# An attention-and-experts kernel: the second layernorm's root, reciprocal and shift once for two blocks, and the expert numbers read into registers in two loads

## What is computed

```python
logits = x @ Wr + br
gate   = max(softmax(logits));  idx = argmax(logits)
xn     = layernorm(x) * ln_g + ln_b
h      = relu(xn @ W1[idx] + b1[idx])      # 128 -> 512
y      = (h @ W2[idx] + b2[idx]) * gate    # 512 -> 128
out    = layernorm(x + y)                  # (v - mean) / sqrt(var + 1e-5)
```

## Time and profile before

| | us |
|---|---|
| median of 3 timed runs | 200.94 |
| lowest, highest of them | 200.79, 201.41 |
| the profiled execution's own time | 202.25 |
| its span | 200.5 |
| busy in the span: PE, PEld, DVE, ACT, POOL | 147.8, 118.1, 161.1, 148.1, 114.3 |
| last DVE instruction starts | 191.4 |
| last OUT on ACT starts | 191.6 |
| last store on POOL starts | 193.4 |

### The profile page before, as it was taken

One profiled execution on the slowest core, in us unless ns is written; L12 is line 12 of the kernel. 1 busy time (PEld: TensorE's weight loads), 2 busy tenths in 40 slices (PEclk: granted clock), 3 DMA queues, 4 the chain that ended last, 5 costly groups with the idle time before them and its releaser, 6 DMA issues.

```text
span 200.5 us, 5489 instructions
## 1 busy us (share of the span) xinstructions
PE 147.8 (74%) x1446; PEld 118.1 (59%) x1446; DVE 161.1 (80%) x819; ACT 148.1 (74%) x448; POOL 114.3 (57%) x200
## 2 busy tenths in 40 slices
PE   0068979988997795922369878998998997999400
PEld 0015736857566474821316767987888996888200
DVE  2455287999998869699698899999999999799900
ACT  2358979997975696527645887999999999898520
POOL 4323140508789765634469215768677687578650
PEclk9999999999999998585556999999999999999955
DMA  5997184000101101101342212223222222110000
GB/s 131 346 394 261 26 273 159 3 0 15 40 26 35 42 29 41 54 15 40 77 126 83 56 30 55 66 71 76 65 75 64 66 64 69 53 54 19 28 9 0
DMA packets 16415, 15.74 MB, mean 79 GB/s; under 512 B 2810, under 2 KB 13142, under 8 KB 16386
## 3 DMA queue, kind: packets, MB, share of 16 engines
q1 hardware_dynamic: 14034, 11.10, 19.0%
q0 software_dynamic: 2272, 4.27, 6.4%
q10 hardware_dynamic: 80, 0.03, 0.1%
HBM read 10.52 MB, written 5.33 MB: 79 GB/s over the span
## 4 chain that ended last, share of the span: by engine, by line
PE 43%; DVE 33%; issue 8%; ACT 6%; DMA 3%; ACTq 2%; POOLq 1%; SPq 1%; POOL 0%; DVEq 0%
PE bank L473 7%; DVE hl L1239 6%; PE bank L592 6%; PE bank L430 5%; PE bank L445 4%; DMA XN<-in_attn_embeddings 3%; DVE z L1248 3%; PE bank L502 3%; PE bank L580 3%; PE bank L576 2%; PE bank L578 2%; DVE zpart L1244 2%; PE bank L579 2%; PE bank L595 2%; DVE bn L1252 2%
## 5 line engine op out<-in xcount | busy, mean ns | idle before, releaser
L418 POOL DMA_INDIRECT out<-OUT,tok x39 | 40.5, 1039 | 26.5 <-issue 25.0
L383 POOL DMA_INDIRECT rows<-R,place x32 | 31.8, 994 | 18.0 <-DVE place L919 9.4
L592 PE MATMUL bank<-W2hl,hh 128*128 x156 | 32.6, 274 | 7.0 <-issue 3.2
L576 PE MATMUL bank<-sel,bias 96*128 96x128 bf16 x156 | 34.6, 222 | 0.0
L578 PE MATMUL bank<-xh,W1h 128*128 128x128 f16 x156 | 34.2, 219 | 0.0
L580 PE MATMUL bank<-xh,W1l 128*128 128x128 f16 x156 | 34.1, 218 | 0.0
L579 PE MATMUL bank<-xl,W1h 128*128 128x128 f16 x156 | 34.0, 218 | 0.0
L1239 DVE SCALAR_TENSOR_TENSOR hl<-bank,hh 128x512 f16<-128x512 f32 x39 | 26.9, 690 | 3.5 <-ACT hh L746 2.6
L595 PE MATMUL bank<-W2hl,hl 128*128 x156 | 27.9, 219 | 0.0
L746 ACT ACTIVATE hh<-bank 128x512 f16<-128x512 f32 x39 | 23.1, 593 | 6.1 <-PE bank L580 5.8
L359 POOL TENSOR_TENSOR rmag<-guarded,minus_half 128x4 f32<-128x4 f32 x8 | 8.2, 1022 | 27.0 <-ACT guarded L615 27.0
(11 more groups left out here) (197 smaller groups left out, 459.3 us busy)
## 6 DMA issues: line engine op xcount, KB each, us to landing
XR<-rows SPq DMA_DIRECT2D x39, 66.0 KB
W<-in_ffn_W SPq DMA_DIRECT2D x1, 2048.0 KB, 11.0
X<-in_attn_embeddings SPq DMA_DIRECT2D x2, 512.0 KB, 8.6
X<-in_attn_embeddings SPq DMA_DIRECT2D x1, 768.0 KB
out<-OUT,tok POOLq DMA_INDIRECT x39
rows<-padt SPq DMA_DIRECT2D x9, 66.0 KB
XN<-in_attn_embeddings SPq DMA_DIRECT2D x2, 256.0 KB, 7.9
rows<-R,place POOLq DMA_INDIRECT x32
```

The lines of the kernel that those rows point to most:

```text
L383: pool.indirect_dma_start(out=rows[:, :], out_offset=bass.IndirectOffsetOnAxis(ap=place[u][:, k:k + 1], axis=0), in_=R[u][:, k, :], in_off ...
L418: pool.indirect_dma_start(out=out[:, :], out_offset=bass.IndirectOffsetOnAxis(ap=tok[k][:, 0:1], axis=0), in_=OUT[k][:, :], in_offset=None ...
L576: pe.matmul(h, bias3[:, c * P:(c + 1) * P], sel, start=True, stop=False)
L592: pe.matmul(y[:, 0:2 * D], hh[k][:, c * P:(c + 1) * P], w, start=c == 0, stop=False)
```

## The change

It does three things.

1. `sd` and `mv2` become tiles for two blocks (`GR = 2`). ACT takes the root, and DVE the reciprocal and the shift, once for both, 128x2 instead of 128x1, in the round in which the second of the two came up before. Block 38 has no partner and stays alone. Mean and variance (mv) are still made block by block.
2. Since the first block of a pair is now ready one round later, OUT on ACT and the store on POOL move by one round for every block: lead -4 instead of -3. The wait for the earlier store of the same buffer moves from the root to OUT.
3. PE reads the expert numbers in two loads, of 16 in front of block 0 and of 23 in front of y of block 12, into 39 registers. The loads in front of blocks 4, 20 and 28 go.

```diff
-            steps([(-3, store), (3, token)])
+            steps([(-4, store), (3, token)])
...
-            held_expert = [pe.alloc_register(f"expert{i}") for i in range(2 * UN)]
+            held_expert = [pe.alloc_register(f"expert{i}") for i in range(NB)]
...
-                if k == UN // 2 and (count(0) + 1) * UN < NB:
-                    if (count(0) + 1) * UN == NB1:
-                        pe.wait_ge(s["tabled"], TABLE_2)
-                    load_experts((count(0) + 1) * UN)
-
-            load_experts(0)
+                if count(0) * UN + k == NB1 - 4:
+                    pe.wait_ge(s["tabled"], TABLE_2)
+                    load_experts(NB1, NB2)
+
+            load_experts(0, NB1)
...
             def b_sd(count, k):
+                n = members(count, k)
+                if n:
+                    act.wait_ge(every["mv"], blocks(count(0), k))
+                    act.activation(sd[k // GR][:, 0, 0:n], mv2[k // GR][:, 0:n, 1], ACT.Sqrt, bias=epsc[:, 0:1]).then_inc(every["sd"], 1)
+
+            def b_fin(count, k):
                 after(act, stored[k], count(0) * 16)
-                act.wait_ge(every["mv"], blocks(count(0), k))
-                act.activation(sd[k][:, 0:1], mv2[k][:, 1:2], ACT.Sqrt, bias=epsc[:, 0:1]).then_inc(every["sd"], 1)
...
-            steps([(5, b_xs), (1, b_hh), (-3, b_fin), (4, b_xt), (-2, b_sd), (4, b_xh)])
+            steps([(5, b_xs), (1, b_hh), (-4, b_fin), (4, b_xt), (-2, b_sd), (4, b_xh)])
...
             def b_rec(count, k):
-                dve.wait_ge(every["sd"], blocks(count(0), k))
-                dve.reciprocal(sd[k][:, 1:2], sd[k][:, 0:1]).then_inc(every["rec"], 1)
+                n = members(count, k)
+                if n:
+                    dve.wait_ge(every["sd"], group(count, k))
+                    dve.reciprocal(sd[k // GR][:, 1, 0:n], sd[k // GR][:, 0, 0:n]).then_inc(every["rec"], 1)
```

More of the change, by code:

```diff
@@ L42 @@
 UN = 8
+GR = 2
 NB1, U1 = 16, 6
@@ L194, in build @@
         bn2 = [sb(f"bn2{i}", [P, 6]) for i in range(UN)]
-        mv2 = [sb(f"mv2{i}", [P, 2]) for i in range(UN)]
-        sd = [sb(f"sd{i}", [P, 3]) for i in range(UN)]
+        mv2 = [sb(f"mv2{i}", [P, GR, 2]) for i in range(UN // GR)]
+        sd = [sb(f"sd{i}", [P, 3, GR]) for i in range(UN // GR)]
         OUT = [sb(f"OUT{i}", [P, D]) for i in range(UN)]
@@ L254, in blocks, with members, group @@
             return turn * UN + k + 1
+        def members(count, k):
+            n = count(0) * UN + k
+            return n % GR + 1 if n % GR == GR - 1 or n == NB - 1 else 0
+        def group(count, k):
+            return (count(0) * UN + k) // GR + 1
         def pads(eng, first, n):
@@ L748, in b_sd @@
             def b_sd(count, k):
-                after(act, stored[k], count(0) * 16)
-                act.wait_ge(every["mv"], blocks(count(0), k))
-                act.activation(sd[k][:, 0:1], mv2[k][:, 1:2], ACT.Sqrt, bias=epsc[:, 0:1]).then_inc(every["sd"], 1)
-            def b_fin(count, k):
-                act.wait_ge(every["shift"], blocks(count(0), k))
-                act.activation(OUT[k][:, :], z[k][:, :], ACT.Identity, scale=sd[k][:, 1:2], bias=sd[k][:, 2:3]).then_inc(every["out"], 1)
-            steps([(5, b_xs), (1, b_hh), (-3, b_fin), (4, b_xt), (-2, b_sd), (4, b_xh)])
+                n = members(count, k)
[3 more added lines that the diff above has]
+            def b_fin(count, k):
+                after(act, stored[k], count(0) * 16)
+                act.wait_ge(every["shift"], group(count, k))
+                scale, shift = (sd[k // GR][:, row, k % GR:k % GR + 1] for row in (1, 2))
+                act.activation(OUT[k][:, :], z[k][:, :], ACT.Identity, scale=scale, bias=shift).then_inc(every["out"], 1)
+            steps([(5, b_xs), (1, b_hh), (-4, b_fin), (4, b_xt), (-2, b_sd), (4, b_xh)])
         @block.vector
@@ L1254, in b_mv @@
             def b_mv(count, k):
[L1256 to L1258 removed]
+                dve.wait_ge(every["bn"], blocks(count(0), k))
+                dve.bn_aggr(mv2[k // GR][:, k % GR, :], bn2[k][:, :]).then_inc(every["mv"], 1)
             def b_rec(count, k):
[L1261 to L1262 removed]
+                n = members(count, k)
+                if n:
+                    dve.wait_ge(every["sd"], group(count, k))
+                    dve.reciprocal(sd[k // GR][:, 1, 0:n], sd[k // GR][:, 0, 0:n]).then_inc(every["rec"], 1)
             def b_shift(count, k):
[L1265 to L1266 removed]
+                n = members(count, k)
+                if n:
+                    dve.wait_ge(every["rec"], group(count, k))
+                    stt(sd[k // GR][:, 2, 0:n], mv2[k // GR][:, 0:n, 0], -1.0, sd[k // GR][:, 1, 0:n], ALU.mult, ALU.mult).then_inc(every["shift"], 1)
             steps([(1, b_hl), (-1, b_mv), (0, b_z0), (-2, b_rec), (0, b_z), (-2, b_shift), (0, b_bn), (0, b_table), (4, b_xl), (4, b_split)])
```

7 lines of the change are left out of this document (3 added, 4 removed).

## The result

The changed kernel took **208.43 us** (median of four runs, 206.62 to 210.14) beside 201.18 for the kernel before. The ratio of the runs is 1.032, 95% interval [1.022, 1.042]; it leaves out the slowest, 210.14 us, which counts as a slow execution. Two later studies gave 1.0413 [1.0366, 1.0459] and 1.0291 [1.0233, 1.0349]. So it is slower, as forecast, but by 3 to 4% and not by 0.9%: 202.8 was predicted, and the range ended at 203.3.

A forecast was written before the change was run, and what follows sets the result against it. ACT was taken to set the pace of the steady rounds. Roots -0.3, loads -0.7, start +0.6, block 12 +1.0 and end +1.3 made +1.9 on 200.94, so 202.8 us; 8-in-10 range 200.5 to 203.3.

The forecast's parts named there:

- Reciprocal and shift: DVE, one of each fewer per two blocks: they run while DVE waits for its own results, so 0 us.
- Root: ACT, one root fewer per two blocks: 0.02 to 0.03 us a pair over about 12 pairs, -0.3 us.
- The end: POOL's last stores: four follow instead of three, 1.28 us apart, so the last starts later, +1.3 us.
- The start: First load, 16 numbers instead of eight, before block 0: longer load and register instructions, nothing hiding them, +0.6 us.
- Block 12: PE's load of 23 in front of y, its room already used up: the longer stall goes through, +1.0 us.
- Blocks 20 and 28: PE's loads removed there: stalls of 0.32 and 0.4 us go, 1.0 more taken as profile-only, -0.7 us together.
- Rival B: Block 28's long stall is in every run, so removing its load wins 1.0 us more: 201.8 us, chance 0.17.
- The move: OUT and store one round later: free in the middle, the token copy one store's time of about 1 us behind.
- Rival A: PE's loads take the same time whatever the number of registers: 201.6 us, chance 0.20.
- C: Load time independent of number, and block 28's 1.4 us stall in every run and removed: 200.5 us, chance 0.13.
- D: Fewer instructions save their whole place on DVE and ACT, 0.09 us a round, 2.2 us: 200.9 us, chance 0.10.
- two signs that I named for being wrong: Last store keeps its distance from hl of block 38, or the steady round gets shorter than 1.86 us.

The follow-up runs named there:

- pairs_16_tok_fours: Kernel before plus pairs and the later OUT and store, sixteen token-number buffers instead of eight, and expert loads of four throughout: ratio 0.9965.
- e9: Kernel before with expert numbers loaded four at a time throughout, the last load four instead of three: ratio 0.9919.
- e4: Kernel before with only OUT and the store one round later, roots block by block, loads of eight: ratio 1.0144.
- e1: Kernel before with only the two long loads of 16 and 23 expert numbers: ratio 1.0074.
- start_16_only: Kernel before with 16 expert numbers loaded at the start and 8, 8 and 7 at blocks 12, 20 and 28: ratio 1.0027.
- e2: Changed kernel with the five loads of the kernel before, so pairs and the later OUT and store alone: ratio 1.0146 in four runs.
- pairs_again: Changed kernel with the five loads of the kernel before, same as e2, measured again in a later study: ratio 1.0196.

## Why the prediction was wrong

The sign was right, and so was what the small operations are worth. By its own steps:

- **Reciprocal and shift: 0 forecast, 0 found.** zpart to z is 0.35 us without the reciprocal, as in the earlier trace rows.
- **Root: -0.3 forecast, -0.3 found** between hl of block 14 and 34 (37.41 us in pairs_16_tok_fours, 37.73 in e9), of which the last rounds give 0.1 back.
- **The end: +1.3 forecast, 1.34 found,** in every trace with pairs, by the step as told: one store more in the row of 1.28 us each. With single roots the move alone costs 0.75 there (e4), so the other 0.6 comes from the pairing: block 34's OUT waits for the pair's shift.
- **The start: +0.6 forecast,** 0.5 by the timed runs (1.0027, whose interval holds 0 to 1.2), 0.5 to 1.3 by the traces. Right in size.
- **Block 12: +1.0 forecast, +2.0 found** in round 14 (4.26 us in e1 against 2.26 in start_16_only), 3.5 where the clock falls. The mis-sized term is the load: "about 1.5 us" became 2.19. The slope of 0.055 a number came from one pair of rows, four and eight numbers on SP; on PE it is 0.07 to 0.08, and the three numbers beyond a multiple of four added 0.7 (20 take 1.51, 23 take 2.19).
- **Blocks 20 and 28: -0.7 forecast, -1.3 found** (44.97 us in e1 against 46.30 in start_16_only from hl of block 14 to 38). The step "I take it that this 1.0 us is missing in the timed runs" was wrong. The longest load was no accident of that execution: it is the one with seven numbers, and it was 1.09 to 1.17 us long in every kernel that kept it. Behind it the round of block 30 took 2.68 to 2.73 us in the five other traces, 0.8 over a round, so of the 1.41 us of the earlier trace rows some 0.8 is in every run and 0.6 was that execution's own, for a reason that is open. Rival B had half of it right.
- **The move: "In the middle this costs nothing" is the step that failed, and it carries most of the miss.** I saw that the token copy now stands one round behind the store that it waits for, and called the next store's own time of about 1 us enough. No row gave a landing time, and I put none in its place. It is 2.1 to 2.9 us and every fourth time 3.0 to 3.95, the copy comes 2.8 behind, and hh, which had 0.2 to 0.4 us of room behind the copy, passes the rest on to hl and the whole round. Found: +1.1 to +3.2 us between hl of block 14 and 38 (e2 and pairs_again against start_16_only), and in the changed kernel +1.2 to +3.8 against e1. In the timed runs the sixteen buffers take back 1.4 to 2.6%, 2.8 to 5.3 us, of the 3.9 to 6.4 us by which the sum was too low. In the first profiled execution, the fastest, the forecast for the profile was +0.9 and first load to last store took 4.3 longer. Of the 3.4 us between, 1.8 lie where the waits are (-0.56 from block 14 to 38 where the forecast had -0.3 - 1.7, and +0.39 ahead of block 13), 0.8 at block 12 and 0.7 at the start.

The sum with these sizes: start 0.6, block 12 and the two loads 0.7, the middle 1.2 to 3.8, the first rounds 0.4 (the wait of block 10), the end 1.3 makes 4.2 to 6.8, and a fall of the clock 1.5 more. The changed kernel was 5.8 to 8.3 us slower by its three ratios.

Rival A (no dependence on the number) is refuted by 0.33 us for four and 1.69 for 24 numbers; C fell with it, and D by pairs_16_tok_fours. Neither of the two signs that I named for being wrong came up, though the forecast was wrong: the last store is 1.3 us farther behind hl of block 38, and the undisturbed rounds average 1.865 us, not less than 1.86. The list of signs lacked the one that mattered, POOL's cg with idle time ended by a landing.

The Trainium skill, page Runtime: NRT & Kernel Launch, section Instruction fetch mechanics, has 200 ns a register, and the page's Terms describe such a load as reading from HBM; here the numbers lie in a tile in SBUF. In fours the runs show 0.07 to 0.08 us a number, and its figure is only near for the numbers left over. Estimated with 0.2 us a register the load of 23 would be 4.6 us; it was 2.19. The Trainium skill, page DMA: Bandwidth & Descriptors, section Latency and other measured facts, puts a floor of about 600 ns under such a load and says that the compiler unrolls four times. Four numbers took 0.33 us, so no floor of that height, but the four is seen.

## What to carry to other kernels

When a step moves later, list every buffer that it lets go of and who waits for it, its DMA's landing included; where the profile has no landing time, zero is the wrong value: bound it by a transfer that has one, and ask for the longest landing and not the usual one (here 3.95 us, once 4.4, against 2.3). An operation that runs in the shadow of its neighbour's own dependency is worth nothing removed, however often; ask first what the fusion delays. A load of registers in front of the engine's critical instruction is best short and often (four numbers, 0.33 us, ten times: 0.8% faster), where the engine's own room hides it, and rounded up to a multiple of four.

## What the runs showed of the hardware

- PE's register load: about 0.3 us for each four numbers, and 0.7 to 0.9 us more for three left over. Loading eight instead of seven, or four instead of three, is faster (0.66 against 1.09 us, 0.34 against 0.81).
- Of every fourth indirect store the last data packet and its report mostly start 2.0 to 3.4 us behind the store's start, where the others have all started within about 2.0, so that landing comes 0.7 to 1.6 us later (3.0 to 3.95 us against 2.3). The trace of before shows it too, and there the wait for it was covered. Why one in four is open.
- TensorE's granted clock fell to 0.50 (1.2 GHz) for 3.4 us behind a standstill of 2.6 to 2.7 us in two traces and stayed at 1.00 behind the same standstill in four. What decides between them is open.
